# Attention scores as two half-height products, and a new order of the slot on TensorE and ScalarE

## What is computed

```python
zn  = layernorm(layernorm(x)) * scale + bias          # two norms in a row
q, k, v = zn @ w_qkv                                  # 16 heads of 16
att = softmax(q @ k.T / 4)                            # 4 batches x 16 heads x 1024 x 1024
x1  = x + layernorm(layernorm(x) + (att @ v) @ w_proj + b_proj)
sh  = ln(silu(y @ sw1 + b1) * (y @ sw2 + b2)) @ sw3 + b3      # y = layernorm(x1), all rows
out = x1 + layernorm(sh, with 512 routed rows mixed with one of 8 experts)
```

## Time and profile before

| | |
|---|---|
| median of 3 runs | 1157.95 us (1154.42 to 1162.0) |
| time of the profiled execution | 1154.46 us |
| its span, first to last instruction | 1152.6 us |
| mean granted TensorE clock | 0.953 |
| slots with value products and maxima (96.97 to 984.03) | 887 us |
| slots after the last maxima (984.03 to 1009.82) | 26 us |

### The profile page before, as it was taken

How to read it: one execution, slowest core, us unless ns; L and a number is a source line. 1 busy time by engine, 2 the same in 40 slices (tenths; PEclk the granted TensorE clock), 3 DMA queues, 4 the chain that set the end, 5 groups by cost and what they waited for, 6 DMA issues and landing times. The chain is left out here.

```text
span 1152.6 us, 14462 instructions
## 1 busy us (share of the span) xinstructions
PE 999.8 (87%) x5348; PEld 391.4 (34%) x5348; DVE 870.8 (76%) x1766; ACT 600.5 (52%) x699; POOL 239.9 (21%) x293
## 2 busy tenths in 40 slices
PE   4378999999899999898899898999798989937983
PEld 2122242222234333232344232322232423226762
DVE  5296978998778768898678868879598798255745
ACT  3015766676665555656556655666455556811010
POOL 4031000201433202135203201141332001602102
PEclk9687999999999999999899999999899999987996
DMA  9806110340430102500711006213601000231001
GB/s 170 114 6 69 38 38 1 55 56 1 61 88 28 46 1 33 80 29 9 112 35 38 2 1 74 37 38 49 99 2 37 1 1 1 74 129 36 1 1 55
DMA packets 46518, 50.27 MB, mean 44 GB/s; under 512 B 8416, under 2 KB 39408, under 8 KB 46064
## 3 DMA queue, kind: packets, MB, share of 16 engines
q1 hardware_dynamic: 45104, 47.51, 22.4%
q10 hardware_dynamic: 960, 0.79, 0.6%
q0 software_dynamic: 384, 1.05, 0.3%
HBM read 13.94 MB, written 8.91 MB: 20 GB/s over the span
## 5 line engine op out<-in xcount | busy, mean ns | idle before, releaser
L1040 DVE TENSOR_REDUCE mx<-ring 128x1 f32<-128x512 f32 x1024 | 648.1, 683 | 150.3 <-PE ring L806 145.3
L654 ACT ACTIVATE prob<-sc 128x1024 f32<-128x1024 f32 x512 | 496.2, 1021 | 337.3 <-PE sc L820 337.2
L806 PE MATMUL ring<-kp,qp 48*128 48x512 bf16 x1024 | 237.0, 394 | 64.4 <-DVE mx L1040 19.5
L834 PE MATMUL obank<-prob,vaug 128*32 128x512 f32 x2048 | 276.3, 612 | 0.7 <-ACT prob L654 0.7
L820 PE MATMUL sc<-qp,kp 112*128 112x512 bf16 x1024 | 270.3, 386 | 5.8 <-DMA qp<-mp 5.0
L806 PEld LDWEIGHTS ring<-kp,qp 48*128 48x128 bf16 x1024 | 60.2, 93 | 404.6 <-DVE mx L1040 193.9
L820 PEld LDWEIGHTS sc<-qp,kp 112*128 112x128 bf16 x1024 | 84.2, 98 | 121.4 <-issue 47.9
L493 POOL TENSOR_SCALAR parts<-resid 128x1024 bf16<-128x1024 f32 x14 | 14.7, 1050 | 388.4 <-DVE resid L1030 388.4
L719 PE MATMUL ring<-ident,zn 128*128 128x128 f32 x128 | 23.5, 326 | 44.2 <-DVE zn L991 19.9
L834 PEld LDWEIGHTS obank<-prob,vaug 128*32 128x32 f32 x2048 | 40.5, 108 | 62.3 <-issue 55.1
L727 PE MATMUL ring<-w,yT 128*128 128x256 f32 x192 | 47.9, 391 | 1.8 <-ACT yT L581 1.8
(11 more groups left out here) (177 smaller groups left out, 734.9 us busy)
## 6 DMA issues: line engine op xcount, KB each, us to landing
kp<-parts SPq DMA_DIRECT2D x96, 128.0 KB, 5.6
qp<-parts SPq DMA_DIRECT2D x180, 64.0 KB, 4.7
x_sb<-x SPq DMA_DIRECT2D x7, 1024.0 KB, 10.4
x_scratch<-x SPq DMA_DIRECT2D x4, 1024.0 KB, 4.4
out<-hid SPq DMA_DIRECT2D x4, 1024.0 KB, 4.4
kp<-ew SPq DMA_DIRECT2D x1, 2048.0 KB, 8.3
x_sb<-x SPq DMA_DIRECT2D x2, 512.0 KB, 4.6
qp<-mp SPq DMA_DIRECT2D x64, 4.0 KB, 1.7
```

The costliest lines, as they stand in the source:

```text
L654: nc.scalar.activation(prob[:, e % 2, 2 * a:2 * a + 2, :].rearrange("p g n -> p (g n)"), sbuf2[a][:, :], ACT.Exp, scale=0.25).then_inc(s_f ...
L806: nc.tensor.matmul(dst[:, :], qp[rows, qh, h, qt * P:(qt + 1) * P], kp[rows, h, kh * HALF:(kh + 1) * HALF], start=True, stop=True).then_in ...
L834: ins = nc.tensor.matmul(obank[i * VW:(i + 1) * VW, :], vaug[:, b % 2, kt, c0:c0 + VW], prob[:, v % 2, i, :], start=(kt == 0), stop=(kt == ...
L1040: nc.vector.tensor_reduce(mx[:, u % 2, n:n + 1], src[:, :], AX.X, ALU.max).then_inc(rv_free, 1)
```

## The change

The 112-row score product becomes two half steps. The first adds the three largest products (and the maxima rows) of one head, the second the rest; within a half step one head uses rows 0 to 63 and its neighbour rows 64 to 111, in different banks. A half step of the second kind waits for a new semaphore, `s_largest`, which the first one of the same buffer raises, since both write the same banks from different rows. On TensorE the slot's order is now: items, first half step of buffer 0, first maxima pair, second half step of buffer 0, both half steps of buffer 1, second maxima pair, value product. In slots from 256 on, without maxima, the order is first half steps of both buffers, then second half steps. On ScalarE the ring items come ahead of the exponentials. "mt" and "ot" keep their place at the end of the slot, which is now behind the value product.

```diff
+        s_largest = sem("largest_products_summed")
@@ scalar, slot loop
+                for key in RING_AT[t]:
+                    if key[0] in BY_ACT:
+                        ring_item(key)
                 if 0 <= e < NS:
                     for a in range(2):
...
                     sc.wait_ge(s_av, 8 * u + 8)
                     nc.scalar.activation(oT[:, u % 2, :], obank[:, :], ACT.Copy).then_inc(s_oT, 1)
-                for key in RING_AT[t]:
-                    if key[0] in BY_ACT:
-                        ring_item(key)
@@ tensor
-                def scores(a):
+                def scores(a, largest):
                     u, kt = e // 8, e % 8
                     g, qh = u % HU // NH, u % NH
-                    dst = open_s(2 * e + a)
                     if e == 0 and a == 0:
                         pe.wait_ge(s_fixed, 32)
-                    if kt == 0 and a == 0:
+                    if kt == 0 and a == 0 and largest:
                         pe.wait_ge(s_mrow[u % 2], 32 * (u // 2 + 1))
-                    for j in range(2):
-                        h = g * GH + 2 * a + j
-                        ins = nc.tensor.matmul(dst[:, j * HALF:(j + 1) * HALF], kp[0:KM, h, kt * P:(kt + 1) * P],
-                                               qp[0:KM, qh, h, :], start=True, stop=True)
-                    ins.then_inc(s_full, 1)
+                    if largest:
+                        dst = open_s(2 * e + a)
+                    else:
+                        dst = sbuf2[a]
+                        pe.wait_ge(s_largest, 2 * e + a + 1)
+                    for low in range(2):
+                        j = low if largest else 1 - low
+                        h, rows = g * GH + 2 * a + j, slice(64 * low, 64 + KR * low)
+                        ins = nc.tensor.matmul(dst[:, j * HALF:(j + 1) * HALF], kp[rows, h, kt * P:(kt + 1) * P],
+                                               qp[rows, qh, h, :], start=largest, stop=not largest)
+                    ins.then_inc(s_largest if largest else s_full, 1)
@@ tensor, slot loop
-                if 0 <= e < NS:
-                    scores(0)
-                    scores(1)
                 for key in RING_AT[t]:
                     if key[0] not in ("max", "mt", "ot"):
                         ring_item(key)
-                if t < NS:
+                if 0 <= e < NS and t < NS:
+                    scores(0, True)
                     max_products(range(0, 2))
+                    scores(0, False)
+                    scores(1, True)
+                    scores(1, False)
+                    max_products(range(2, 4))
+                elif 0 <= e < NS:
+                    scores(0, True)
+                    scores(1, True)
+                    scores(0, False)
+                    scores(1, False)
+                elif t < NS:
+                    max_products(range(0, 4))
                 if 0 <= e - 1 < NS:
                     value_product(e - 1)
-                if t < NS:
-                    max_products(range(2, 4))
```

## The result

The changed kernel takes 1169.4 us (median of 4, 1165.83 to 1171.03) against 1157.39 for the kernel before in the same comparison: ratio 1.0096, 95% interval 1.0061 to 1.0132. It is slower by 12 us.

The account below looks back on a forecast made before the run. TensorE was taken to set plain slots (2.61 us), VectorE those with statistics. Costs and savings, including -23.6 for late reads, summed to +10.7 us: 1165.2 on the profiled execution, 1168.7 on the median; range 1147 to 1205.

Parts of the forecast that it names:

- Changes of shape: On TensorE, two of a plain slot's four tile-shape changes go, -0.2 us; with an item only one, -0.1.
- The wait of PE for PE: Half step to half step through `s_largest` takes 0.44 us, not 0.22: covered for buffer 0, +0.22 for buffer 1.
- The fourth maximum's bank as a floor: In plain slots the fourth maximum needs the first's bank, free 1.15 us after M; TensorE arrives after 1.10: slot 2.69.
- Plain slots: The 51 plain slots of 2.61 us grow by 0.08 each to 2.69, +4.1 us.
- Items: Slots with items grow: q/k +0.25 us each, v +0.17, p and h +0.12, transposes +0.17, w slots 0.
- ScalarE's late reads: TensorE's idle time before maxima products, waiting for ScalarE's reads of ring items, goes entirely: -23.6 us.
- Waits for GpSimd: Nine TensorE waits for GpSimd grow by 0.97 us each, as scores now stand behind the wait: +8.7 us.
- Slots without maxima: The 12 slots without maxima grow from 2.15 to 2.69 us, 0.54 each: +6.5 us.
- the early reads pay twice: Rival, chance 0.22: TensorE's waits for VectorE go along with the late reads, up to -22.0 us more: 1147 us.
- The wait is long: Rival, chance 0.15: TensorE sees its own semaphore after 0.25 us instead of 0.05, lengthening half-step waits; priced 1203 us.
- the loads show: Rival, chance 0.10: 98 ns weight loads show before half steps and M in the same rows, +34 us: 1203 us.
- The change doesn't do what it says: Rival, chance 0.03: the two heads of a half step don't run together on TensorE, +200 us: 1367 us.

Follow-up runs that it names:

- experiment 4: Changed kernel with the first half step of buffer 1 ahead of the second of buffer 0, so no wait stands open: 1161.4 us, ratio 1.0043.
- experiment 6: Changed kernel with VectorE reducing only half of each maxima bank: 1125.3 us, ratio 0.971.
- experiment 7: Changed kernel with buffer 1's first half step ahead of buffer 0's second, and only half of each maxima bank reduced: 1108.6 us, ratio 0.958.
- half maxima: VectorE reduces only half of each maxima bank, in the kernel before (1115.9 us) and in the changed kernel (1125.3 us).
- experiment 3: Kernel before with items first on TensorE and ScalarE, scores in one 112-row piece, second maxima pair still behind the value product: 1177.0 us, ratio 1.0169.
- experiment 8: Changed kernel, but in slots without maxima both half steps of buffer 0 come before those of buffer 1: 1169.1 us, ratio 1.0085.
- experiment 9: Kernel before, TensorE unchanged; ScalarE reads transposes between the exponentials, other items after them but ahead of the oT copy: 1143.8 us, ratio 0.987.
- experiment 2: Changed kernel with ScalarE's items behind the exponentials again, but ahead of the oT copy: 1408.4 us in one run.

## Why the prediction was right

It was right in sign and size, but the size owes something to luck. Its steps one by one:

- *Changes of shape* (step 1): right. Half step to M takes 0.22 to 0.23 where scores to M took 0.31.
- *The wait of PE for PE* (step 3): 0.45 where I had 0.44, worked out from TensorE's answers to VectorE and ScalarE. Covered for buffer 0, open for buffer 1, as said.
- *The fourth maximum's bank as a floor*: right, 2.70 against 2.69, and experiments 4, 6 and 7 show both halves of it. What I had not put beside it is that ScalarE's chain gives 2.70 too as soon as the waits are covered.
- *Plain slots*: of the 51 of 2.61, 45 take 2.70, as said. Six carry VectorE's work that moved by a slot and take 3.04 to 3.84, while the other 48 slots without an item, mt or ot, which the forecast held at 0, lost 13.6 us in sum: late reads that showed there, and VectorE's work.
- *mt slots*: 2.91 where I had 2.89, but in 9 slots only. There are 18 with mt alone and not 15, the others take 3.54 or 4.02 with VectorE's work, and the kind grew by 1.4 us where I had -3.0.
- *Items*: too small. q/k slots lost 0.29 (4.33 to 4.62), not 0.25; v 0.29, not 0.17; p and h 0.22, not 0.12; w slots 0.2 (3.47 to 3.64 before, 3.83 after), not 0; transposes 0.21, not 0.17. That w slots are VectorE's was wrong in part: with half maxima they take 3.47 before and 3.72 after, so TensorE's own cycle grew past what VectorE had set. By my counts that is 24 x 0.04 + 12 x 0.12 + 24 x 0.10 + 12 x 0.2 + 42 x 0.04 = +8.9 us. What failed is the term "V to item is a change too", priced 0.10: the change costs twice that, since the first matmuls behind it take 0.10 longer as well (that it is the first weight load is my reading). Four q/k matmuls behind scores took 1.88; behind V they take 1.98.

The q/k item before and after, as the timelines of the two kernels have it:

```profile
265.44 1.88 PE L749 MATMUL ring<-zT,wk 128*128 128x512 f32 x4
```

```profile
196.51 1.98 PE L750 MATMUL ring<-zT,wk 128*128 128x512 f32 x4
```

- *ScalarE's late reads*: 23.6 became 4.5, so 19.1 went: I had 4.5 too much.
- *Waits for GpSimd*: the step that failed. I had "GpSimd's end hangs on DVE's statistics slots earlier and doesn't move, so each such wait grows by 0.97", +8.7; measured +2.1 (15.8 to 17.9). The same x item in the changed kernel and in experiment 3, to set beside the earlier trace rows:

```profile
650.70 0.66 PE L720 MATMUL ring<-ident,zn 128*128 128x128 f32 x4 [1.94 <-POOL zn L460]
```

```profile
656.98 0.66 PE L719 MATMUL ring<-ident,zn 128*128 128x128 f32 x4 [3.03 <-POOL zn L459]
```

Experiment 3 also puts the scores behind the item but keeps the second M behind V, and its wait grows by 0.97. In the changed kernel the second M comes a value product (1.00) earlier in the slot, and all six waits of x and u fell by 0.12 (2.06 to 1.94, 1.19 to 1.07). My reading: VectorE finishes its maxima, and the statistics behind them, and with these GpSimd starts, about that much earlier against the value product. It fits that the one wait ahead of the first value product, where M has nothing to overtake, grew the same in both (2.09 to 3.91). But the two kernels differ in the half steps too; no run has moved M alone.
- *Slots without maxima*: +5.8 for 6.5, and experiment 8 shows that their order sets them.

The sum again, with what was measured: 10.7 + 8.9 (items) + 4.5 (late reads) - 6.6 (GpSimd) - 0.7 (slots without maxima) = 16.8. From this go PE's waits of mt and ot for a maximum, 4.0 before and absent after (a part was counted in the mt slots), and 1.8 of the wait for the maxima's DMA, 5.0 to 3.2: about 11, and the measured span grew by 11.4. This is bookkeeping with chosen terms and no proof: it leaves out the plain and mt slots above, and the 2.5 by which M's waits for VectorE grew. What the starts of the value products give without a choice is this, for the 242 slots up to the last maxima:

| slots, from V to V | number | before, us | changed, us | difference |
|---|---|---|---|---|
| without item, mt or ot | 99 | 292.22 | 288.53 | -3.69 |
| mt alone | 18 | 58.11 | 59.55 | +1.44 |
| ot alone | 13 | 46.60 | 47.44 | +0.84 |
| q/k or v item | 36 | 167.23 | 169.01 | +1.78 |
| p or h item | 24 | 108.68 | 113.78 | +5.10 |
| w item | 12 | 45.38 | 48.33 | +2.95 |
| transposes | 40 | 166.33 | 162.65 | -3.68 |
| all | 242 | 884.55 | 889.29 | +4.74 |

The forecast was good to 1 us because terms that were 13 short (items, late reads) met terms that were 7 over and some 6 that weren't listed; by its terms it was good to about 10.

The rivals: "the early reads pay twice" is refuted: PE's waits of M for VectorE rose from 19.5 to 22.0, and only the 4.0 of mt and ot went. "The wait is long" and "the loads show" are refuted by 0.45 for the waiting half step, and 0.22 between free half steps in the same rows. The weight loads stay hidden in 64-row tiles as in 112-row ones. So for same-row neighbours the rule of the Trainium skill quoted in the forecast (TensorE: Matmul & The Clock Gate, Part 3, The mechanism) does not hold here: 0.22 apart with loads of 0.09. "The change doesn't do what it says" is refuted too: the two heads of a half step are listed in 0.39, the time of one.

## What to carry over

When instructions change places on one engine, move every one of them against the others' queues: the pair that moved ahead of the value product made an early read necessary (239 us without it, in one run) and at the same time, by my reading, cancelled waits that the moved scores would have added. Before paying for shorter steps on the engine that looks full, find the buffer that limits it next: here three ring banks and two score buffers gave 2.70 in plain slots with the wait open and with it covered. A read that comes late was repaired most cheaply here at the reader, item by item (experiment 9, 1.3%), without touching the busy engine.

## What the runs showed of the hardware

- TensorE answers its own semaphore as fast as another engine's: 0.45 from start to start where the matmul is listed with 0.39, so 0.06 behind the listed end, where it answers ScalarE after 0.05 and VectorE after 0.06.
- A change of tile shape costs 0.10: 0.31 from the last score matmul to M, against 0.22 from half step to M. The Trainium skill, TensorEngine Tiling (Array Packing), Key Properties, says that a change of tiling mode drains the engine; the 0.31 against 0.22 agrees. Where an f32 item follows the change, its first matmuls take another 0.10 (q/k item 1.88 to 1.98). A bf16 half step or M behind V does not: it is listed with 0.39 and comes 1.00 after V, as ever.
- Two half-height matmuls in different rows and banks start together (two in 0.39) and take one step of 0.22, also when they add to what the bank holds.
- Behind waits of 1.9 us in most slots with an item (experiment 2) the granted clock of the slots was 0.91 instead of 0.99. So a wait on TensorE cost more than its own length there: 164.5 us of waits, and some 88 us more of busy time.
